# The last expert's tiles 28 to 30 in seven block products, and the output without the last expert made between tiles

## The reference, cut to what matters

```python
x = x + ga * attn(h)                       # attention, 16 heads, window 128
h = _layernorm(x) * (1 + cb) + sb
gate = einsum('btd,edf->ebtf', x, Wg)      # e = 8 experts, d = f = 256
up   = einsum('btd,edf->ebtf', x, Wu)      # (experts 0, 1 also get low-rank terms)
mid  = silu(gate) * up
out  = einsum('ebtf,efd->ebtd', mid, Wd)
x = x + gb * einsum('bte,ebtd->btd', weights, out)
```

## Time and profile before

| | |
|---|---|
| median of 3 executions | 797.65 us (797.46 to 798.36) |
| the profiled execution | 797.38 us |
| its span, first to last instruction | 795.6 us |
| granted TensorE clock | 0.999 of full speed |
| busy: TensorE | 783.7 us, 98% |
| busy: VectorE | 549.2 us, 69% |
| busy: ScalarE | 509.3 us, 64% |
| busy: GpSimd | 453.2 us, 57% |

### The profile page before, as it was taken

One profiled execution on the slowest core, in us unless ns is written; L12 is line 12 of the kernel. 1 busy time (PEld: TensorE's weight loads), 2 busy tenths in 40 slices (PEclk: granted clock), 3 DMA queues, 4 the chain that ended last, 5 costly groups with the idle time before them and its releaser, 6 DMA issues.

```text
span 795.6 us, 15708 instructions
## 1 busy us (share of the span) xinstructions
PE 783.7 (98%) x5404; PEld 716.5 (90%) x5404; DVE 549.2 (69%) x1138; ACT 509.3 (64%) x1355; POOL 453.2 (57%) x595
## 2 busy tenths in 40 slices
PE   9899999999999999999999999999999999999997
PEld 8688899999999999999999998999888899999987
DVE  5677676475567567558558658767786688888876
ACT  5877677577677767667757776552554566766522
POOL 3777587476567567657657658232325562332096
PEclk9999999999999999999999999999999999999999
DMA  8300020000000000000000000200700101100002
GB/s 332 110 28 1 2 61 1 1 8 1 1 7 2 1 1 8 1 2 7 2 1 8 1 1 1 108 1 1 199 7 35 40 1 41 36 6 1 2 0 107
DMA packets 8766, 23.43 MB, mean 29 GB/s; under 512 B 1640, under 2 KB 4328, under 8 KB 8560
## 3 DMA queue, kind: packets, MB, share of 16 engines
q1 hardware_dynamic: 7824, 21.82, 8.3%
q10 hardware_dynamic: 864, 0.61, 0.2%
HBM read 19.79 MB, written 2.64 MB: 28 GB/s over the span
## 4 chain that ended last, share of the span: by engine, by line
PE 93%; DVE 2%; ACT 2%; issue 2%; POOL 1%; DVEq 0%; POOLq 0%; ACTq 0%
PE ps_o L736 14%; PE ps_proj L613 9%; PE ps_proj L615 9%; PE ps_proj L614 9%; PE ps_s L613 7%; PE ps_s L614 7%; PE ps_s L615 7%; PE ps_turn L665 4%; PE ps_y L613 4%; PE ps_y L614 4%; PE ps_y L615 4%; PE ps_turn L683 3%; PE ps_turn L613 2%; PE ps_turn L614 2%; PE ps_turn L615 2%; PE ps_o L615 2%
## 5 line engine op out<-in xcount | busy, mean ns | idle before, releaser
L1133 ACT ACTIVATE ps_s<-ps_s,knorm 128x512 f32<-128x512 f32 x128 | 79.2, 657 | 95.7 <-PE ps_s L615 95.5
L736 PE MATMUL ps_o<-vaug,probs 128*128 128x129 f32 x1024 | 135.3, 275 | 1.7 <-POOL probs L1983 0.9
L736 PEld LDWEIGHTS ps_o<-vaug,probs 128*128 128x128 f32 x1024 | 129.1, 191 | 8.0 <-POOL probs L1983 1.4
L1521 DVE RECIPROCAL rden<-ps_o 128x2 f32<-128x2 f32 x128 | 21.8, 170 | 152.7 <-PE ps_o L736 152.6
L1491 DVE TENSOR_TENSOR prod<-ps_proj,cs 128x1024 f32<-128x1024 f32 x76 | 92.5, 1218 | 11.0 <-ACT sq L1076 11.0
L1934 POOL TENSOR_TENSOR root<-ssq,powers 128x4 f32<-128x4 f32 x76 | 77.8, 1024 | 27.6 <-ACT sq L1076 27.6
L1076 ACT ACTIVATE sq<-ps_proj 128x128 f32<-128x128 f32 x304 | 80.1, 279 | 18.0 <-PE ps_proj L615 15.2
L1981 POOL TENSOR_SCALAR_AFFINE_SELECT probs<-probs 128x256 f32<-128x256 f32 x64 | 26.4, 412 | 105.9 <-ACT probs L1141 105.6
L1950 POOL TENSOR_TENSOR prod<-prod 128x512 f32<-128x512 f32 x62 | 80.1, 1292 | 9.7 <-DVE prod L1491 9.7
L613 PE MATMUL ps_proj<-w_hi,h_hi 128*128 128x512 f32 x192 | 83.1, 433 | 0.9 <-DVE w_lo L1434 0.5
L1989 POOL TENSOR_TENSOR we_lo<-raw_e,we_hi 128x512 fp32r<-128x512 f32 x22 | 28.7, 1320 | 85.8 <-DVE mid_seven L1632 62.0
(11 more groups left out here) (309 smaller groups left out, 2426.2 us busy)
## 6 DMA issues: line engine op xcount, KB each, us to landing
raw_e<-in_we SPq DMA_DIRECT2D x8, 768.0 KB, 4.3
raw_p<-in_wqkv SPq DMA_DIRECT2D x6, 512.0 KB, 8.3
raw_e<-in_wo SPq DMA_DIRECT2D x4, 512.0 KB, 11.5
x_all<-in_x SPq DMA_DIRECT2D x1, 1536.0 KB, 7.9
out<-acc SPq DMA_DIRECT2D x3, 512.0 KB, 2.6
x_all<-in_wmod SPq DMA_DIRECT2D x1, 1024.0 KB, 9.8
gates_a<-gate_rows_dram SPq DMA_DIRECT2D x8, 128.0 KB, 2.9
gates_b<-gate_rows_dram SPq DMA_DIRECT2D x1, 1024.0 KB, 10.8
```

What stands on the lines that cost most here:

```text
L736: mm = pe.matmul(ps_o[:, h * (D + 1):(h + 1) * (D + 1)], probs[:, s % 2, at:at + P], vaug[b % 2][:, k, i // 2, :], start=(h == 0 and k == ...
L1133: act.activation(ps_s[:, t, :], ps_s[:, t, :], ACT.Tanh, scale=knorm[:, b % 2, t, i // 2:i // 2 + 1]).then_inc(tanh_done, 1)
```

## The change

`EIGHT` is now 31: the tiles 28, 29 and 30, three of the last expert's four, take the form of seven block products, and only tile 31 keeps eight. The weight sums, their rounding and their rests are made for expert 7 too, at tiles 25 and 26. `rest_of_output(n)` for n = 0 to 3 is called within GpSimd's loop, at the steps 27, 28, 29 and 30, so each starts only when `mid_done` of that tile is there; `last_part` stays behind the loop. The three `part` buffers lie in other places, since the place of before is now used by the sums, and VectorE has three waits for these places to be free. The TensorE wait ahead of the first tile in eight products asks for both products of the tile before it (`mid_done` 2 x `EIGHT`), where it asked for those of the tile before that: the chain of tile 30 lies in `ps_s`, which this tile writes first. Lines of the changed kernel are 2 higher than before up to VectorE's `accumulate` and 6 higher in GpSimd's functions.

```diff
 
 
 
-SEVEN, EIGHT = FIRST_OF[NL + 1], FIRST_OF[NE - 1]
+SEVEN, EIGHT = FIRST_OF[NL + 1], len(TILES) - 1
 
 EXPERT_STEPS = {FIRST_OF[2] - 2: [(2, 0), (2, 1)], FIRST_OF[2] - 1: [(2, 2)], FIRST_OF[2] + 1: [(3, 0), (3, 1)], FIRST_OF[3] - 1: [(3, 2)]}
 EXPERT_STEPS |= {FIRST_OF[e - 1]: [(e, 0), (e, 1)] for e in range(NL + 2, NE)}
 EXPERT_STEPS |= {FIRST_OF[e] - 1: [(e, 2)] for e in range(NL + 2, NE)}
 
-SUMS_S = {FIRST_OF[e] - 3: e for e in range(NL + 1, NE - 1)}
-ROUND_S = {FIRST_OF[e] - 2: e for e in range(NL + 1, NE - 1)}
-REST_S = {FIRST_OF[e] - (1 if e == NL + 1 else 2): e for e in range(NL + 1, NE - 1)}
+SUMS_S = {FIRST_OF[e] - 3: e for e in range(NL + 1, NE)}
+ROUND_S = {FIRST_OF[e] - 2: e for e in range(NL + 1, NE)}
+REST_S = {FIRST_OF[e] - (1 if e == NL + 1 else 2): e for e in range(NL + 1, NE)}
 
 SUMS_T = {SEVEN - 4: 2, SEVEN - 2: 3}
 ROUND_T = {SEVEN - 4: [0], SEVEN - 3: [1], SEVEN - 1: [2, 3]}
+
+REST_OUT = {FIRST_OF[NE - 1] - 1 + n: n for n in range(NT // 4)}
 REST_T = {SEVEN - 4: 0, SEVEN - 2: 1, SEVEN - 1: 2, SEVEN: 3}
 SLOT_SUMS = {63: 0, 64: 1}
 STEPS = 27
@@ -397,7 +399,7 @@
         quarters = place("quarters", [P, 2, 4, S], F32, prod_at)
         h2_dram = nc.dram_tensor("h2_dram", (P, 2, KT, S), F32, kind="Internal").ap()
 
-        part = [place(f"part{n}", [P, 2, TT, E], F32, probs_at + BLOCK // 2 + n * BLOCK) for n in range(LATE)]
+        part = [place(f"part{n}", [P, 2, TT, E], F32, offset) for n, offset in enumerate((wo_at + 3 * BLOCK, raw_at, k_at[1] + BLOCK))]
 
         raw_o = raw_e[:].rearrange("p a m f -> p (a m f)").rearrange("p (r k n) -> p r k n", r=RAW_RING, k=KT)
 
@@ -782,7 +784,7 @@
                     pe.wait_ge(h2_split, 1 + max(BATCH_OF_H2.index(b) for b in (2 * n, 2 * n + 1)))
                 pair = up_pair(g)
                 if g == 2 * EIGHT:
-                    pe.wait_ge(mid_done, 2 * EIGHT - 2)
+                    pe.wait_ge(mid_done, 2 * EIGHT)
                     pe.wait_ge(c21_added, EIGHT - SEVEN)
                 elif g == 2 * EIGHT + 1:
                     pe.wait_ge(c11_added, EIGHT - SEVEN)
@@ -1674,9 +1676,13 @@
                 dve.wait_ge(router, STEPS * (n + 1))
                 if e == NE - 1 and n == LATE:
                     dve.wait_ge(base_done, 2 * n + half + 1)
+
                 if e == NE - 1 and n == 0 and half == 0:
-
-                    dve.wait_ge(low_ready, 3 * NL)
+                    dve.wait_ge(gu_ready, 4 * LAST_OF[e - 1] + 4)
+                if e == NE - 1 and n == 1 and half == 0:
+                    dve.wait_ge(we_split, 3 * (NE - 2) + 2)
+                if e == NE - 1 and n == 2 and half == 0:
+                    dve.wait_ge(t_split, 6)
                 for t in range(2):
                     at_t = 2 * half + t
                     w = r_wf[:, 4 * n + at_t, e:e + 1]
@@ -2119,9 +2125,8 @@
                     rest_t(REST_T[m])
                 if m in SUMS_T:
                     sums_t(SUMS_T[m])
-            for n in range(LATE):
-                rest_of_output(n)
-            rest_of_output(LATE)
+                if m in REST_OUT:
+                    rest_of_output(REST_OUT[m])
             for n in range(LATE):
                 last_part(n)
             for at_t in range(2):
```

## The result

The changed kernel took 800.29 us (median of nine runs, 799.25 to 802.14), the kernel before 798.08 beside it (nine runs, 797.29 to 798.83). The ratio is 1.0034, 95% interval [1.0024, 1.0044]: slower, by 2.2 us. The profiled execution took 800.97 us: a span of 798.5, which is 2.9 more than before, and 2.47 around it (1.78 before).

The account below looks back on a forecast made before the run. TensorE's 1.5 us saving is lost to VectorE's waits for GpSimd, whose tail sets the end: T(30) 779.7 + 16.5 = 796.2, + 3.1 = 799.3 span, + 1.78 = 801.1 us; range 798.4 to 803.0.

Parts of the forecast that it names:

- Part 1: TensorE's work: tiles 28 to 30 save 1.65 us, the last expert's sums cost 0.15; net -1.50 us.
- T(27): End on VectorE of the first of tile 27's last two products; forecast 754.2 us with the sums' 0.15.
- Part 2, tile 28: GpSimd against VectorE: five GpSimd operations, the fifth holding until T + 7.42; T(28) comes 9.27 us after T(27).
- Part 2, tiles 29 and 30: GpSimd against VectorE: four GpSimd operations each, as in tile 13; 8.1 us taken for each tile, 8.04 up to 8.25.
- T(30): End on VectorE of the first of tile 30's last two products; forecast 779.7 us, 777.6 at TensorE's pace.
- the rival in which it does not wait: C22 and L1624 on VectorE don't wait for GpSimd: T(30) = 778.3, time 799.7 us; chance 10%.
- the one in which each tile loses a whole operation: Last GpSimd operation ahead of C22 in each new tile: T(30) = 782.1, time 803.5 us; chance 8%.
- The rival that VectorE's slack swallows the collisions: TensorE keeps its pace, T(30) = 777.6, only GpSimd's tail is longer: 799.0 us, not tellably slower; chance 17%.
- Part 3: GpSimd's tail: 16.5 us from T(30) to its last add at 796.2, then 3.1 to the span's end.
- TensorE's wait at tile 31: Sign: TensorE waits at the head of tile 31 for VectorE's product just after T(30).
- the vanished pause of GpSimd: Sign: GpSimd loses its idle 3.53 us before the last part, its last add ending about 3.7 later than 792.48.
- the pair near 3 us: Sign: VectorE's two mid_lo of tile 31 take near 3 us, against 1.47 before.

Follow-up runs that it names:

- no outputs at all: Changed kernel with the output without the last expert left out, 16 GpSimd operations fewer: 797.36 us against 797.37 for the kernel before (1.0001).
- one tile earlier: Changed kernel with the last expert's down weights rounded and their rest made one tile earlier: 800.47 us against 797.31 for the kernel before (1.0049).
- one operation fewer: Changed kernel without the residual added to the second half of token tiles 0 to 2: 799.63 us against 797.31 for the kernel before (1.0031).
- the short tail: Changed kernel with four of GpSimd's last adds left out (token tiles 0 and 1): 797.98 us against 797.37 for the kernel before (1.0012).
- the kernel with free outputs: Changed kernel with the output without the last expert made in one piece, not waiting for tiles 28 to 30: 804.63 us against 797.37 before (1.0091).
- two tiles in seven products: Changed kernel with only tiles 28 and 29 in seven products, last expert's down weights one tile earlier: 798.25 us against 797.31 before (1.0011).
- the placement alone: Kernel before, tiles 28 to 31 in eight products, only each output piece waiting for its tile's first product: 797.48 us against 797.37 (1.0005).
- both versions with two tiles in seven products: Only tiles 28 and 29 in seven products, 798.25 us; the same with token tile 0's last part accumulated on VectorE, its output last, 797.48 us.

## Why the prediction was right

The forecast was 801.1 us; 800.29 was measured. The sign and the place of the loss were as forecast, and so was the mechanism, but for tiles 29 and 30. The size is less well met than the two times suggest: 3.7 us over the profiled execution were forecast, the span grew by 2.9 and the median by 2.2 (over 798.08, where the forecast knew 797.65). Against the profiled execution's span the steps stand so:

- **Part 1.** The last expert's sums were to cost 0.15 us: T(27) comes 120.66 us after the step of tile 12 instead of 120.51, 0.15. The saving of 1.50 on TensorE measured 1.32 (no outputs at all): three new tiles took 23.48 there instead of 23.40, and three old ones 25.00 (779.75 less the 754.75 of the earlier trace rows) instead of 25.05, which is 0.13 of the 0.18.
- **Part 2, tile 28.** Forecast 9.27, measured 9.11. The cause was that the fifth operation starts just before C22: shown by both moves, one tile earlier (7.94) and one operation fewer (8.04, the figure that the forecast took from tile 13). Most of the 0.16 comes from a reading: the prediction has mid_lo end as a GpSimd operation ends, but in tile 13 it ends at 639.49, 0.55 behind the operation's end at 638.94. With 0.55 in place of C22's full 0.68 behind the fifth operation the sum is 9.14.
- **Part 2, tiles 29 and 30.** The term most out of size: 8.1 each forecast, 7.87 measured. I had taken C22 as issued at T + 6.19 and free, at best, so 8.04 was the least. In fact the two mid_lo took only 0.89 and 1.19 there: the first was issued at T + 1.04, 0.34 before GpSimd's first operation ended, where in tile 28 it was issued at T + 1.41, just behind the start of the second. C22 is then issued at T + 4.95, waits, and ends 0.55 after GpSimd's fourth operation. From T on: 6.16 to the end of that operation, 0.55 to the end of C22, 1.16 to the next T, which starts GpSimd again: 7.87. It is a ring of two engines, 0.07 longer than TensorE's mean pace of 7.80, and 0.06 over two tiles than the same tiles without outputs (7.81 and 7.87). So nearly all of the lag at T(30) is tile 28's. With C22 caught in all three tiles, the rival in which it does not wait fell, and with 7.87 the one in which each tile loses a whole operation.
- T(30) came at 779.14 instead of 779.7, and TensorE started tile 31 145.90 us after the step of tile 12 instead of 146.21 before: 0.3 of the 1.5 us was left, where the forecast left nothing. TensorE did wait there for the product just after T(30), 0.7 us. The rival that VectorE's slack swallows the collisions asked for T(30) at most 0.2 us behind TensorE's pace: 754.29 + 23.4 = 777.69, and it was 1.45.
- **Part 3.** From T(30) to GpSimd's last add 16.5 us forecast, 16.23 measured (795.37); from there to the end 3.1 and 3.13. VectorE ended 0.58 earlier, at 794.79 (forecast 795.1), its last pair at 2.86 instead of 3.49. The collisions in the tail lengthened GpSimd's work by 1.66 (16.23 less 14.57), where 1.92 was forecast. That GpSimd sets the end, and that the last pair is caught beside it, are shown together by the short tail: 2.95 us less. How much each would be alone isn't: that kernel takes away both, and the two ends lie only 0.58 apart.

The span was forecast at 799.3 and was 798.5: 0.1 for T(27), -0.6 for the tiles, -0.3 for the tail. The profiled time was nearer (800.97) only because 2.47 us lay around the span instead of 1.78; that is luck, and nothing in the forecast is to be credited for it.

Of the signs named for the profile after, TensorE's wait at tile 31, the vanished pause of GpSimd and the pair near 3 us are there. Three were too large: C22 is 1.08 us over its 0.68, not 1.3; the last add comes 2.9 us after 792.48, not 3.7; and ScalarE's step L1230 of tile 28 comes 8.38 us after that of tile 27 (751.50 and 759.88), 0.6 over the pace and not 1.4, since the step stands ahead of C22 in its tile.

The Trainium skill (page "SBUF — State Buffer", section "SBUF: two separate sides") has VectorE and GpSimd exclude each other on their shared port pair for a whole instruction, where VectorE reads both inputs from SBUF and the GpSimd operation reads SBUF too. The runs agree for C22: 1.76 us beside a GpSimd operation, 0.68 without it, and for L1626 and L1634 in the kernel with free outputs (1.78 and 1.30).

## What to carry to other kernels

Work that one engine does "beside" another is free only between the operations that exclude each other; before moving it, write down when the other engine issues those operations, and let the moved work end ahead of them or start behind. A wait that delays one piece of an engine's work delays the whole queue behind it, so the pause ahead of the last piece (3.53 us here) is the most that such a move may use. It is no guarantee: 1.38 of it used in eight-product tiles cost nothing, 2.12 used with two tiles in seven products cost 0.76 us of stage, because GpSimd's adds had come beside VectorE's last pair. And where two engines start each other, their ring has its own pace, which has to be compared with the bounding engine's.

## What the runs showed that I had not expected

Programs with the same instructions in their first 630 us reach tile 12 up to 3.5 us apart. The busy time and granted clock of TensorE in two stretches (columns: length; busy and count of PE, PEld, DVE, ACT, POOL; clock; DMA share; GB/s), the kernel before and the one without outputs:

```profile
10.00:15.00 5.00, 4.60 (x28) 3.89 (x27) 3.88 (x5) 4.15 (x13) 0.27 (x1) 1.00 1.02 417
40.00:50.00 10.00, 8.93 (x60) 8.04 (x61) 7.46 (x17) 6.66 (x17) 6.59 (x12) 1.00 0.01 3
```

```profile
10.00:15.00 5.00, 5.00 (x26) 4.70 (x25) 3.78 (x4) 3.42 (x6) 0.00 (x0) 0.68 1.02 413
40.00:50.00 10.00, 7.85 (x42) 6.94 (x41) 6.67 (x15) 4.94 (x15) 5.97 (x12) 0.83 0.03 4
```

The clock was granted at 0.68 and 0.83 in the second, so part of each stretch ran at the lower of its two levels, 1.2 instead of 2.4 GHz, and at 1.00 in the first. The stretch from 40 to 50 us sorts all eleven profiles. Where it shows 1.00 (the kernel before, both profiles of the changed one, the one with an operation left out) the step of tile 12 comes at 632.55 to 633.63; where it shows 0.83 (the other seven) at 634.38 to 636.02. What decides it I don't know: in the ten microseconds ahead TensorE was busy 8.00 us both in the kernel before and in the placement alone, and only the second then had 0.83. Nor is it all: with the outputs free the step came at 636.02, and 10 to 15 us shows 1.00 there.

The times hold a second thing that no stage shows. Around the span lay 1.69 to 1.81 us in every execution whose span is on record of the kernel before, of the placement alone and of both versions with two tiles in seven products; in the six kernels with three such tiles it was 1.7 to 2.9, on the mean 1.95 to 2.5. That puts 0.2 to 0.8 us on their times, and its cause is open.

Both are as large as an effect of 0.1%. Set against the kernel before, the stage of the changed kernel says 2.8 us more and its times say 2.2 and 4.5; in every other kernel here the time lies 0.1 to 1.9 us above what the stage says. So the stages show how the work of the last tiles shifts, and the times decide whether a kernel is faster: by them none of the versions here beats the kernel before.
